# Two small loads of a fused FFN kernel issued from ScalarE instead of SyncE

## The chip, the cores and the metric

The kernel runs on one core of one Trainium2 chip. A core has five engines with instruction streams of their own: TensorE (PE in the profile, its weight loads PEld), VectorE (DVE), ScalarE (ACT), GpSimd (POOL) and SyncE (SP). They meet through semaphores. DMAs are issued by SyncE, GpSimd or ScalarE and carried by the core's 16 DMA engines. The metric is the time of one execution on the device in microseconds (us); lower is better.

## The reference

For each of 32 batch entries (here: tiles) of a 128 x 2048 input, a small MLP turns a conditioning vector into a softmax over 8 experts; the 8 expert matrices (128 x 128) are mixed with it and applied to the tile, with a mixed bias. A quantized SwiGLU feed-forward block (gate, up, down) follows, and its result is added to the input.

```python
h = gelu(embedding @ W0 + b0)
h = gelu(h @ W1 + b1)
att = softmax((h @ W2 + b2), axis=-1)                  # 32 x 8
agg_w = einsum('bk,koi->boi', att, weight[..., 0])     # mixed experts
out = einsum('boi,bih->boh', agg_w, x) + (att @ bias_k)[:, :, None]
# then, on 4096 rows of 2048: q, s = dynamic_quant(row * inv)
inter = clip(silu(gate(q)) * up(q))                    # 2048 -> 1024
x = x + down(dynamic_quant(inter))                     # 1024 -> 2048
```

## The kernel before, in words

Five instruction streams are written out by hand, one function per engine inside `adaln_ffn`; each stream's order is the order of its lines, and waits on named semaphores join them. A tile is one batch entry: 128 rows of 2048. For each tile TensorE runs conv (mixed expert matrix times input, L566), gate and up products (L613) and down (L716), interleaved over neighbouring tiles.

The start is the part that matters here. SyncE's stream opens with its loads, L340 to L352: `mlp_s` (L340: the conditioning vectors, the MLP's matrices and biases in one block of 153 KB), `b2_s` (L341: the 8 logit biases, copied to all 128 partitions), `wexp` (L342: the expert matrices, 512 KB, one row of 4 KB per partition), input 0 (L343, 1 MB), `invg_bc` (L344, 1 MB, one row copied to all partitions), inputs 1 and 2 (L345, L346), four row loads (L347 to L350) and, behind a wait for the first gate weights, input 3.

With the MLP block there, TensorE computes the two hidden layers (L511, L514) with ScalarE's Gelu between them (L920, L922). TensorE then waits for b2 (L516) and adds it with a one-row matmul (L518), logits follow (L521, L523), VectorE takes the maximum (L1016, L1018) and ScalarE the exponential (L924). The mixed expert matrix of tile 0 is made by two engines: VectorE sums experts 0 to 4 (`dve.wait_ge(wexp_in, 16)`, then L1069, L1072), TensorE experts 5 to 7 (L537) with diagonal matrices from ScalarE (L833), and VectorE adds both (L1077). ScalarE scales the experts for tile 1 (L837). conv(0) waits for that sum and for input 0. VectorE's bias sum (L1045) releases GpSimd's diagonal matrix (L461); GpSimd then waits for input 0 and issues the four gate weight loads (L432).

ScalarE's stream begins with a wait for the first hidden product and the Gelu. The compiler puts a table load (ACT_TABLE_LOAD) in front of that, and another one in front of the exponential. ScalarE issues no DMA. While TensorE waits early on, it runs filler matmuls (L505) whose result nobody reads.

Of the kernel before, what the change touches and what calls it, by code (L numbers as in the profile page):

```python
# [5 lines left out]
def adaln_ffn(nc, x, mlp, b2, weightT, w_gateT, w_upT, w_downT, inv_gate, rows, out):  # L6
# [6 lines left out]

    P = 128
    B, _, H = x.shape
    K = b2.shape[0]
    HID = 128
# [15 lines left out]
    with ctx:  # L33
        def sb(name, shape, dt=fp32):
            return ctx.enter_context(nc.sbuf_tensor(name, shape, dt))
# [4 lines left out]
        def sem(name):  # L40
            return ctx.enter_context(nc.semaphore(name))
# [10 lines left out]
        wexp = sb("wexp", [P, K, P])  # L52
# [70 lines left out]
        def qiT_at(t):  # L123
            if t == B - 1:
                return qgT[:, 0:KI * P]
            return QIT_HOME[t] if t < 2 else qiT[:, :]
# [29 lines left out]
        b2_s = qiT32[:, P + 3 * B:P + 3 * B + K]  # L156
# [35 lines left out]
        b2_in = sem("b2_in")  # L192
        wexp_in = sem("wexp_in")
# [126 lines left out]
        def xslot(t):  # L320
            return xt[:, (t % XS) * H:(t % XS + 1) * H]
# [16 lines left out]
        def _(sp):  # L338

            sp.dma_start(mlp_s, mlp).then_inc(mlp_in, 16)  # L340
            sp.dma_start(b2_s, b2.partition_broadcast(P)).then_inc(b2_in, 16)  # L341
            sp.dma_start(wexp[:, :, :], weightT).then_inc(wexp_in, 16)  # L342
            sp.dma_start(xslot(0), x[0, :, :]).then_inc(x_in[0], 16)  # L343
            sp.dma_start(invg_bc[:, :], inv_gate.partition_broadcast(P)).then_inc(invg_in, 16)  # L344
            sp.dma_start(xslot(1), x[1, :, :]).then_inc(x_in[1], 16)  # L345
# [445 lines left out]
        def _(act):  # L791
# [123 lines left out]
            def fix_i(t):  # L915
                act.wait_ge(iturned, 16 * t)
                nc.scalar.activation(qiT_at(t), qiT_at(t).bitcast(fp16), ACT.Copy, bias=-ROUND).then_inc(qiT_ready, 1)  # L917

            act.wait_ge(hid_mm, 1)
            nc.scalar.activation(h1, hid_ps, ACT.Gelu, bias=b0_s).then_inc(hid_act, 1)  # L920
            act.wait_ge(hid_mm, 2)
# [480 lines left out]
```

## Time and profile before

| | us |
|---|---|
| median of 3 runs | 803.78 (803.5 to 803.93) |
| the profiled execution | 803.78 |
| its span, first to last instruction | 802.0 |
| TensorE busy | 794.1 |
| VectorE busy | 715.4 |
| ScalarE busy | 441.1 |
| GpSimd busy | 147.9 |

A row of the timeline gives start, duration, engine, line, operation and tiles, and in brackets how long the engine sat idle before it and what released it; SPq is SyncE's stream of DMA issues, and its duration is that of the issue, not of the transfer. The chain rows give start, duration and what was on the chain. The time "to landing" runs from the start of an issue to its semaphore. The DMA view cuts a stretch into 40 slices and gives for each the busy tenths of the 16 DMA engines and the rate in GB/s.

### The profile page before, as it was taken

How to read it: one execution, taken by the hardware profiler on the slowest of the kernel's cores; microseconds unless marked ns; L12 is line 12 of the kernel's file. 1: busy time of each engine (PE TensorE's matmuls, PEld its weight loads, DVE VectorE, ACT ScalarE, POOL GpSimd, SP SyncE). 2: the span in 40 equal slices, each digit the busy share in tenths (PEclk: the TensorE clock that was granted, in tenths of full speed). 3: DMA queues.
4: the chain of work that ended last, by engine and by line, in shares of the span. 5: the costliest groups of instructions: out<-in, count | busy, mean ns of one | idle time of the engine just before them, and what ended most of it. 6: DMA issues, size and time to landing. Idle time of an engine off the chain costs nothing.

```text
span 802.0 us, 9186 instructions
## 1 busy us (share of the span) xinstructions
PE 794.1 (99%) x3521; PEld 365.3 (46%) x3521; DVE 715.4 (89%) x810; ACT 441.1 (55%) x385; POOL 147.9 (18%) x138
## 2 busy tenths in 40 slices
PE   8999999999999999999999999999999999999997
PEld 5554444444444444444444444444444444444443
DVE  6897899999888998888998888998888988888968
ACT  7774335555664545664545654555654546655531
POOL 2703210210122220122220122210222210222000
PEclk9999999999999999999999999999999999999999
DMA  8998745454445444445444445445455444454342
GB/s 300 225 215 172 161 142 171 149 166 125 131 138 171 145 145 120 129 145 170 145 145 122 119 154 167 147 145 112 122 161 161 154 129 136 108 167 154 90 111 105
DMA packets 162964, 119.81 MB, mean 149 GB/s; under 512 B 151780, under 2 KB 152164, under 8 KB 153703
## 3 DMA queue, kind: packets, MB, share of 16 engines
q1 hardware_dynamic: 161192, 106.64, 44.6%
q0 software_dynamic: 1728, 12.58, 7.8%
q8 instruction: 28, 0.46, 0.2%
q14 instruction: 16, 0.13, 0.1%
HBM read 60.48 MB, written 33.55 MB: 117 GB/s over the span
## 4 chain that ended last, share of the span: by engine, by line
PE 88%; DVE 7%; ACT 2%; issue 1%; DMA 1%; DVEq 0%; ACTq 0%
PE gate_ps L613 26%; PE up_ps L613 25%; PE down_ps L716 22%; PE conv_ps L566 12%; DVE amax L1092 2%; PE gate_ps L716 1%; DVE region L1150 1%; DVE xt L1265 1%; DVE down_sc L1256 1%; ACT qg L820 0%; DMA qgT<-qg 0%; PE up_ps L566 0%; PE down_ps L571 0%; ACT y L809 0%; DVE region L1219 0%
## 5 line engine op out<-in xcount | busy, mean ns | idle before, releaser
L716 PE MATMUL down_ps<-wd,qiT 128*128 128x512 bf16 x896 | 211.2, 379 | 0.0
L613 PE MATMUL gate_ps<-wg,qgT 128*128 128x512 bf16 x928 | 205.7, 379 | 0.0
L613 PE MATMUL up_ps<-wu,quT 128*128 128x512 bf16 x896 | 202.4, 379 | 0.0
L1092 DVE TENSOR_REDUCE amax<-region 128x1 f32<-128x2048 f32 (+1 forms) x90 | 173.0, 1922 | 1.2
L442 POOL TENSOR_TENSOR prod<-wexp,att_bc 128x1024 f32<-128x1024 f32 x28 | 53.1, 1898 | 540.9 <-DVE region L1150 498.3
L716 PEld LDWEIGHTS down_ps<-wd,qiT 128*128 128x128 bf16 x896 | 87.6, 98 | 123.4 <-issue 28.5
L613 PEld LDWEIGHTS gate_ps<-wg,qgT 128*128 128x128 bf16 x928 | 90.8, 98 | 109.4 <-issue 1.1
L613 PEld LDWEIGHTS up_ps<-wu,quT 128*128 128x128 bf16 x896 | 87.7, 98 | 106.1 <-ACT quT L885 0.4
L820 ACT ACTIVATE qg<-region,recip 128x2048 f16<-128x2048 f32 x30 | 60.1, 2002 | 128.9 <-DVE recip L1102 128.9
L566 PE MATMUL conv_ps<-xt,aggw 128*128 128x512 f32 x244 | 116.9, 602 | 0.8 <-ACT y L809 0.5
L809 ACT ACTIVATE y<-conv_ps,aggb 128x512 bf16<-128x512 f32 x116 | 78.9, 686 | 59.6 <-PE conv_ps L566 55.0
L1256 DVE SCALAR_TENSOR_TENSOR down_sc<-down_ps,scale,swd_bc 128x512 f32<-128x512 f32 x117 | 86.8, 742 | 0.2 <-PE down_ps L716 0.2
L1265 DVE TENSOR_TENSOR xt<-xt,down_sc 128x512 f32<-128x512 f32 x122 | 84.1, 690 | 3.2
L1203 DVE SCALAR_TENSOR_TENSOR region<-up_ps,scale,swu_bc 128x1024 f32<-128x1024 f32 x28 | 35.9, 1283 | 49.7 <-PE up_ps L613 49.7
L917 ACT ACTIVATE qiT<-qiT 128x1024 bf16<-128x1024 f16 x29 | 30.6, 1056 | 80.1 <-DMA qiT<-qi 80.1
L850 ACT ACTIVATE qu<-region,recip 128x2048 f16<-128x2048 f32 x30 | 60.1, 2003 | 18.6 <-DVE recip L1102 18.6
L566 PEld LDWEIGHTS conv_ps<-xt,aggw 128*128 128x128 f32 x244 | 46.3, 192 | 41.5 <-issue 29.8
L1147 DVE TENSOR_TENSOR region<-y,invg_bc 128x2048 f32<-128x2048 bf16 x27 | 61.7, 2284 | 0.0
L1150 DVE TENSOR_TENSOR region<-y,invu_bc 128x2048 f32<-128x2048 bf16 x27 | 61.7, 2283 | 0.0
L879 ACT ACTIVATE qgT<-qgT 128x2048 bf16<-128x2048 f16 x27 | 51.6, 1910 | 6.8 <-DMA qgT<-qg 6.8
L887 ACT ACTIVATE quT<-quT 128x2048 bf16<-128x2048 f16 x27 | 51.3, 1901 | 2.5 <-DMA quT<-qu 2.5
L899 ACT ACTIVATE qi<-region,recip 128x1024 f16<-128x1024 f32 x30 | 34.2, 1141 | 16.5 <-DVE recip L1102 16.5
(180 smaller groups left out, 582.1 us busy)
## 6 DMA issues: line engine op xcount, KB each, us to landing
xt<-x SPq DMA_DIRECT2D x30, 1024.0 KB, 4.8
out<-xt SPq DMA_DIRECT2D x29, 1024.0 KB, 4.0
wg<-w_gateT POOLq DMA_DIRECT2D x4, 1024.0 KB, 17.8
wu<-w_upT POOLq DMA_DIRECT2D x4, 1024.0 KB, 15.0
wd<-w_downT POOLq DMA_DIRECT2D x4, 1024.0 KB, 9.6
xt<-x SPq DMA_DIRECT2D x4, 512.0 KB, 4.8
invg_bc<-inv_gate SPq DMA_DIRECT2D x1, 1024.0 KB, 8.2
out<-xt SPq DMA_DIRECT2D x2, 512.0 KB, 2.9
```

The costliest lines, as they stand in the source:

```text
L442: nc.gpsimd.tensor_tensor(prod[:, :, :], wexp[:, :, :], a, ALU.mult).then_inc(pagg_step, 1)
L566: nc.tensor.matmul(conv_bank(t, c), aggw[t % 2][:, :], xcols(t, c), start=True, stop=True).then_inc(conv_done, 1)
L613: last = nc.tensor.matmul(acc[:, n * BANK:(n + 1) * BANK], codes[:, k * P:(k + 1) * P], wts[:, k, n * BANK:(n + 1) * BANK], start=(k == 0) ...
L716: last = nc.tensor.matmul(down_bank(t, c), qiT_at(t)[:, k * P:(k + 1) * P], wd[:, k, c * BANK:(c + 1) * BANK], start=(k == ks[0]), stop=(k ...
L809: nc.scalar.activation(y_at(t)[:, c * BANK:(c + 1) * BANK], conv_bank(t, c), ACT.Identity, scale=norm, bias=aggb[:, t:t + 1]).then_inc(y_r ...
L820: nc.scalar.activation(qg[:, :], xg_at(t), ACT.Copy, scale=trecip(t, 0), bias=ROUND).then_inc(gcodes_ready, 1)
L850: nc.scalar.activation(qu[:, :], xu_at(t), ACT.Copy, scale=trecip(t, 1), bias=ROUND).then_inc(ucodes_ready, 1)
L1092: nc.vector.tensor_reduce(amax[:, i:i + 1], src, axis=AX.X, op=ALU.max, apply_absolute_value=True).then_inc(max_ready, 1)
L1147: nc.vector.tensor_tensor(region1[:, :], y[:, :], invg_bc[:, :], ALU.mult).then_inc(xg_ready, 1)
L1150: nc.vector.tensor_tensor(region2[:, :], y[:, :], invu_bc[:, :], ALU.mult).then_inc(xu_ready, 1)
L1256: nc.vector.scalar_tensor_tensor(down_sc[c % 2], down_bank(t, c), tscale(t, 2), swd_bc[:, c * BANK:(c + 1) * BANK], ALU.mult, ALU.mult).th ...
L1265: nc.vector.tensor_tensor(result_at(t, c), xcols(t, c), down_sc[c % 2], ALU.add).then_inc(result_ready, 1)
```

## The change

The loads of `b2_s` and `wexp` are taken out of SyncE's stream, where they stood between the MLP block and input 0, and put at the head of ScalarE's stream, before its first wait. They go out through ScalarE's own DMA queue. Their destinations and semaphores stay the same, and so does everything that waits for them.

```diff
@@ -338,8 +338,6 @@
         def _(sp):
 
             sp.dma_start(mlp_s, mlp).then_inc(mlp_in, 16)
-            sp.dma_start(b2_s, b2.partition_broadcast(P)).then_inc(b2_in, 16)
-            sp.dma_start(wexp[:, :, :], weightT).then_inc(wexp_in, 16)
             sp.dma_start(xslot(0), x[0, :, :]).then_inc(x_in[0], 16)
             sp.dma_start(invg_bc[:, :], inv_gate.partition_broadcast(P)).then_inc(invg_in, 16)
             sp.dma_start(xslot(1), x[1, :, :]).then_inc(x_in[1], 16)
@@ -916,6 +914,8 @@
                 act.wait_ge(iturned, 16 * t)
                 nc.scalar.activation(qiT_at(t), qiT_at(t).bitcast(fp16), ACT.Copy, bias=-ROUND).then_inc(qiT_ready, 1)
 
+            act.dma_start(b2_s, b2.partition_broadcast(P)).then_inc(b2_in, 16)
+            act.dma_start(wexp[:, :, :], weightT).then_inc(wexp_in, 16)
             act.wait_ge(hid_mm, 1)
             nc.scalar.activation(h1, hid_ps, ACT.Gelu, bias=b0_s).then_inc(hid_act, 1)
             act.wait_ge(hid_mm, 2)
```

## Rows read from the trace of the kernel before

**Rows 1.** The page: span, busy time by engine, the chain by engine.
```profile
span 802.0 us, 9186 instructions
...
PE 794.1 (99%) x3521; PEld 365.3 (46%) x3521; DVE 715.4 (89%) x810; ACT 441.1 (55%) x385; POOL 147.9 (18%) x138
...
PE 88%; DVE 7%; ACT 2%; issue 1%; DMA 1%; DVEq 0%; ACTq 0%
```
**Rows 2.** The chain in order of time, 0 to 50 us: start, us, what.
```profile
0.73 2.26 DMA region<-mlp
...
6.41 0.24 ACT att_bc L924
...
7.28 1.63 PE gate_ps L537 x6
...
9.01 0.30 DVE aggw L1077
...
9.45 3.53 PE conv_ps L566 x4
```
**Rows 3.** Busy time by stretch: engines, granted clock, DMA share, GB/s.
```profile
9.45:97.00 87.55, 87.30 (x466) 44.61 (x467) 77.10 (x82) 53.13 (x56) 31.73 (x27) 1.00 0.93 208
```
**Rows 4.** The timeline of SyncE's issues, from the start.
```profile
0.73 0.39 SPq L340 DMA_DIRECT2D region<-mlp  x1
1.18 0.42 SPq L341 DMA_DIRECT2D qiT<-b  x1
1.65 0.42 SPq L342 DMA_DIRECT2D wexp<-weightT  x1
2.12 0.43 SPq L343 DMA_DIRECT2D xt<-x  x1
2.59 0.43 SPq L344 DMA_DIRECT2D invg_bc<-inv_gate  x1
```
**Rows 5.** The DMA view, issues up to 3 us: KB each, us to landing.
```profile
region<-mlp SPq DMA_DIRECT2D x1, 153.0 KB, 2.3
qiT<-b SPq DMA_DIRECT2D x1, 4.0 KB, 2.8
wexp<-weightT SPq DMA_DIRECT2D x1, 512.0 KB, 4.2
xt<-x SPq DMA_DIRECT2D x1, 1024.0 KB, 6.3
invg_bc<-inv_gate SPq DMA_DIRECT2D x1, 1024.0 KB, 8.2
```
**Rows 6.** The DMA view in 40 slices, 2 to 3 us, then 3 to 4.
```profile
GB/s 49 147 49 98 98 49 490 98 490 147 490 245 490 245 392 294 297 203 207 161 57 103 53 53 4 3 4 4 3 4 3 1 1 5 3 1 4 166 4 169
DMA packets 208, 0.13 MB, mean 135 GB/s; under 512 B 105, under 2 KB 206, under 8 KB 208
...
GB/s 4 4 4 1 1 9 3 4 4 494 328 4 1 165 3 1 165 0 3 1 3 165 329 0 165 0 1 1 164 0 164 0 0 0 492 328 164 328 328 0
DMA packets 78, 0.10 MB, mean 96 GB/s; under 512 B 55, under 2 KB 55, under 8 KB 78
```
**Rows 7.** The timeline of ScalarE up to its first activation.
```profile
0.72 1.28 ACT L920 ACT_TABLE_LOAD   x1 [0.72 <-PEq L1396]
...
3.71 0.29 ACT L920 ACTIVATE region<-gate_ps,region 128x32 f32<-128x32 f32 x1 [1.70 <-PE gate_ps L511]
```
**Rows 8.** The timeline where b2 and wexp are first used, and the last sum.
```profile
4.61 0.63 PE L518 MATMUL up_ps<-qiT 1*128 1x32 f32 x2
...
6.68 0.29 DVE L1069 TENSOR_SCALAR aggw<-wexp,att_bc 128x128 f32<-128x128 f32 x1 [0.30 <-ACT att_bc L924]
...
9.01 0.29 DVE L1077 TENSOR_TENSOR aggw<-aggw,gate_ps 128x128 f32<-128x128 f32 x1 [0.19 <-PE gate_ps L537]
```
**Rows 9.** The timeline of GpSimd before the gate weight loads.
```profile
9.90 1.90 POOL L461 TENSOR_TENSOR region<-ident,att_bc 128x1024 f32<-128x1024 f16 x1 [8.18 <-DVE aggb L1045]
...
11.74 2.35 POOL L432 DMA_DIRECT2D wg<-w_gateT  x4
```

## Prediction

> **What bounds the kernel now.** I read the page's busy line and chain first. TensorE is busy for 794.1 of 802.0 us, and 88% of the chain that ended last is its matmuls [rows 1]. So a change to a few loads at the start can only pay if TensorE's useful work begins sooner, or if a later stall of it goes. The next view is the chain in order of time: it begins with the DMA of the MLP block (issue to landing 0.73 to 2.99 us), runs through the small MLP, the exponential at 6.41 and the aggregation of expert weights on TensorE at 7.28 and on VectorE at 9.01, and reaches conv(0), the first large matmul, at 9.45 [rows 2]. The table of stretches then shows what stands behind it: between 9.45 and 97 us TensorE is busy for 87.30 of 87.55 us [rows 3]. Two things follow. Whatever moves conv(0) moves the end by the same amount, because there is no idle time to soak it up. And whatever only makes data land sooner after 9.45 is worth at most the 0.25 us of idle time in that stretch. The profiled execution stands at 803.78 us, 1.78 beyond its span of 802.0, and equals the median of the three runs shown, so a shift in the span can be added to 803.78 directly.
>
> **Part 1: two issues leave SyncE.** SyncE issues one DMA per 0.47 us (starts at 0.73, 1.18, 1.65, 2.12, 2.59) [rows 4]. Two go, so input 0 is issued at 1.18 instead of 2.12, and everything behind it, inv_gate, inputs 1 and 2 and the four row loads, up to 0.94 us sooner. Who needs this? Input 0 now lands at 2.12 + 6.3 = 8.4 us [rows 4, 5] and conv(0) starts at 9.45, released by the VectorE sum that ends at 9.31 [rows 2]. It has about 1 us to spare, so its gain is nothing. GpSimd also waits for input 0 before it issues the gate weights, but its diagonal matrix, released by VectorE, runs from 9.90 to 11.80 in front of that, and the first issue is at 11.74 [rows 9]; again nothing. inv_gate lands at 2.59 + 8.2 = 10.8 [rows 4, 5], before y(0) exists. The bulk stream being ahead is worth 0 to 0.25 us; I take 0, the value nearest to what these releasers show.
>
> **Part 2: two issues enter ScalarE ahead of its table load.** ScalarE's first instruction is the table load, 0.72 to 2.00, and its first Gelu starts at 3.71, behind the first MLP matmul [rows 7]. No row shows a DMA issue on ScalarE; the nearest are SyncE's, 0.39 to 0.43 us each at a spacing of 0.47 [rows 4]. Two of them put the table load at 0.72 + 0.94 = 1.66, ending at 2.95, with 0.75 us left before the Gelu. The cover is thus 0.75 us of waiting for the MLP block; it would be gone if one issue took more than about 0.8 us, twice what SyncE's take. Cost: 0. The second table load (for the exponential) is not touched.
>
> **Part 3: the bias row beside the MLP block.** The row (b2) needs 128 tiny packets. In the slices between about 2.65 and 3.7 us the core's DMA engines carry 3 to 5 GB/s most of the time, with 105 packets under 512 B in one microsecond and 55 in the next: that is b2, some 1.25 us long from about 2.45 to 3.7, although it holds next to no bytes [rows 6]. Now it is queued behind the MLP block and cannot hurt it. After the change both are issued at about 0.72, on two queues of the same engines. Bounds: 0, if tiny packets slip between the block's, to +1.25 us, if the whole of b2 goes first; below 0 is excluded since nothing stands before the block now. I take +0.1: the block moves its bytes at 300 to 490 GB/s in the same slices in which b2's first packets already run [rows 6]. b2 itself is wanted at 4.61 and lands at 1.18 + 2.8 = 3.98 [rows 4, 5, 8]; issued earlier it stays in time.
>
> **Part 4: the expert weights beside input 0.** This is the part on the path. The weights (wexp, 512 KB) now land at 1.65 + 4.2 = 5.85 us [rows 4, 5]; VectorE first uses them at 6.68 and then waits 0.19 us for TensorE before the last sum at 9.01 [rows 8], so they may land as late as 6.68 + 0.19 less a few hundredths of reaction, 6.84, before conv(0) moves. TensorE wants them at 7.28 only [rows 2]. Their lead today comes from order: they stand in front of input 0 in one queue. After the change they stand on another queue beside input 0. The rate: input 0 and inv_gate land 10.8 - 8.4 = 2.4 us apart, 1 MB (1.05 million bytes) each, so 0.42 to 0.43 MB/us. The MLP block's bytes are through at about 2.65 and it lands at 2.99, 0.35 later. If packets alternate between the queues (input 0's rows are 8 KB, wexp's 4 KB), wexp gets a third of the rate. When does it start? b2 is in front of it on its own queue; b2's quiet stretch begins at 2.45, 1.27 us after its issue at 1.18, and lasts 1.25 us, so from an issue at 0.72 it ends at 0.72 + 1.27 + 1.25 = 3.25. By then input 0 has moved for 0.6 us, 0.25 MB of its 1.05; the other 0.80 passes with 0.40 of wexp in 1.20/0.42 = 2.85 us, to 6.1, and wexp's last 0.12 takes 0.9 us at a third of the rate beside inv_gate, to 7.0. Landed 7.35, so +0.5 us. The same sum with b2 ending a quarter of a microsecond sooner or later gives some +0.25 or +0.75. I take +0.5. Bounds: 0 (wexp is served first; it then lands no later than its 5.85 of now) to +2.4 us (b2 is stretched until input 0 is through at 2.65 + 2.5 = 5.15, and wexp's 0.52 MB at a third of the rate takes 3.75 more: 8.9, landed 9.25, against 6.84).
>
> The delays of parts 3 and 4 don't add: the block's delay also moves the need for wexp. conv(0) moves by the larger, +0.5. Sum: 0 + 0 + 0.5 on 803.78 gives 804.3 us.
>
> The Trainium skill ("DMA: Bandwidth & Descriptors", section "Queues, rings and completion order") says that each DMA engine switches between queues only at packet boundaries, a packet being typically 9 to 17 descriptors, so a 128-row load's share of one engine would go out whole. By that rule wexp waits for input 0 at most once, the first rival below. The same page's section "Issuing engines are not separate DMA queues" says that issuing from several engines saves only the sequencer's issue time, which speaks against any gain here. No row of this trace shows SyncE's and ScalarE's queues side by side, since ScalarE issues nothing.
>
> **Rivals.**
> - Whole loads in turn, nothing late. Input 0 first, then wexp: 1.57 MB from 2.65 is done at 6.4, landed 6.7, before 6.84. Result 803.8 (803.5 to 804.0). For it: it needs only the bytes and the rate, and lands 0.14 us inside the limit. Against: the limit is close, and any packet of inv_gate or pause of b2 in front of wexp's last row breaks it.
> - The MLP block is late (part 3) by more than 0.2 us and sets the shift: about +0.6, 804.4. For it: b2's packets hold the engines nearly idle for a microsecond. Against: its packets are tiny.
> - On the other side, slower: wexp starved. The mechanism is b2 stretched by input 0's 8 KB packets, so that wexp meets inv_gate instead; it decides once wexp lands after 6.84, and passes 0.2% (1.6 us) at a landing of 8.45. At the bound it gives +2.4, 806.2; I price it at 805.9.
> - Faster: the earlier bulk stream removes idle time of TensorE I don't see as DMA. At most -0.25 in the stretch of [rows 3]; 803.5. A gain above 1.6 us has no row behind it.
> - The change doesn't do what it says: issues on ScalarE are far slower than SyncE's (past 0.8 us each), or a second issuing engine adds time outside the span. Table load and wexp late together: +1 to +2, 805.3.
>
> **How the numbers follow.** Forecast (wexp late by 0.2 to 1.4) 0.42; whole loads in turn 0.24; MLP block late 0.14; starved 0.09; earlier stream 0.05; slow issues 0.06. 0.2% is 1.6 us, about what a measurement of this kernel can tell from no change. Within it lie the forecast, the first two rivals, most of the small gain and half of the slow issues: 0.86. Slower: 0.09 + 0.03 = 0.12 less some starved cases that stay inside, 0.11. Faster: 0.03 for what no row shows. The range 803.2 to 805.7 takes in all but the starved case and part of the last.
>
> **What would show it.** In the changed kernel's timeline: SyncE issues input 0 near 1.2; ScalarE's two issues start near 0.72 and the table load ends before 3.1 with the Gelu still behind TensorE. In the chain: if the MLP block lands by 3.1, part 3 is right; if VectorE's first use of wexp is released by the wexp DMA near 7.3, and not by the exponential, part 4 is right; conv(0) at 9.9 to 10.0 confirms the sum. conv(0) at 9.45 means whole loads in turn. The forecast is wrong if conv(0) stays put and the time still moves by over a microsecond, or if TensorE's idle time between conv(0) and 97 us is no longer near 0.25 us.

## The result and the profile after

| | before | after |
|---|---|---|
| median of 7 runs, us | 803.85 (803.50 to 804.45) | 806.97 (806.15 to 807.79) |
| ratio | | 1.0037, 95% interval 1.0028 to 1.0046 |
| profiled execution, us | 803.78 | 806.23 |
| its span, us | 802.0 | 804.4 |

The change costs 3.1 us by the medians (2.3 to 3.7 by the interval) and 2.4 us between the two profiled executions, all of it inside the span: what lies around it is 1.8 us in both.

The page after, lines that answer to [rows 1]. TensorE's busy time rose by 0.9 us, and a DMA has a percent of the chain by line that it did not have:

```profile
span 804.4 us, 9186 instructions
PE 795.0 (99%) x3521; PEld 365.4 (45%) x3521; DVE 715.3 (89%) x810; ACT 441.1 (55%) x385; POOL 147.8 (18%) x138
PE 88%; DVE 7%; ACT 2%; DMA 2%; issue 1%; ACTq 0%; DVEq 0%
```

The chain after in order of time answers to [rows 2]. It doesn't begin with the MLP block any more but with the expert weights, 1.17 to 8.45 us, and reaches conv(0) at 11.02 instead of 9.45:

```profile
1.17 7.28 DMA wexp<-weightT
...
8.54 0.30 DVE aggw L1069
...
10.61 0.28 DVE aggw L1077
...
11.02 3.75 PE conv_ps L564 x4
```

The stretch of 87.55 us from conv(0) on, as in [rows 3], is as full as it was:

```profile
11.02:98.57 87.55, 87.30 (x463) 44.45 (x464) 76.22 (x82) 52.39 (x53) 31.69 (x27) 1.00 0.89 195
```

The issues, the table load and the first uses, in the timeline after, answer to [rows 4, 7, 8]. The two issues on ScalarE take 0.40 and 0.46 us and the table load ends at 2.94, as worked out. The MLP block is there at 3.78 (3.01 before), and VectorE now waits 1.40 us for the expert weights, where it waited 0.30 for the exponential:

```profile
0.73 0.39 SPq L340 DMA_DIRECT2D region<-mlp  x1
0.73 0.40 ACTq L917 DMA_DIRECT2D qiT<-b  x1
1.17 0.46 ACTq L918 DMA_DIRECT2D wexp<-weightT  x1
1.18 0.42 SPq L341 DMA_DIRECT2D xt<-x  x1
...
1.66 1.28 ACT L920 ACT_TABLE_LOAD   x1 [1.66 <-PEq L1396]
...
3.78 0.17 DVE L1005 COPY qiT<-region 128x8 f32<-128x8 f32 x1 [2.12 <-DMA region<-mlp]
...
8.54 0.29 DVE L1069 TENSOR_SCALAR aggw<-wexp,att_bc 128x128 f32<-128x128 f32 x1 [1.40 <-DMA wexp<-weightT]
```

The DMA view after, 4 to 7 us. q1 is SyncE's queue and carries input 0 in rows of 8 KB; q10 is ScalarE's and carries the expert weights in rows of 4 KB. They move 100 and 95 packets in these 3 us, and in each half microsecond of them 15 to 19 and 15 to 17: the engines take them in turn, row by row, and the expert weights get a third of the bytes (0.39 of 1.21 MB).

```profile
DMA packets 195, 1.21 MB, mean 403 GB/s; under 512 B 0, under 2 KB 0, under 8 KB 95
## 3 DMA queue, kind: packets, MB, share of 16 engines
q1 hardware_dynamic: 100, 0.82, 65.4%
q10 hardware_dynamic: 95, 0.39, 35.8%
```

And 2 to 4 us. Of the 0.31 MB on q1 the MLP block is about a half, and q10 moves little more than the bias row:

```profile
q1 hardware_dynamic: 143, 0.31, 67.9%
q10 hardware_dynamic: 149, 0.02, 6.1%
```

**Where the time between the two records went.** conv(0) starts 1.57 us later, but the second aggregation on TensorE (L537, after L535) starts at 20.36 instead of 17.96, 2.40 later; the last matmul ends up 2.44 later. So 0.83 us arise between the start of conv(0) and the second aggregation, with no wait. The timeline's weight loads show it. Before, they come every 0.86 us until 12.14 and every 0.43 us from 12.81 on:

```profile
11.29 0.34 PEld L566 LDWEIGHTS conv_ps<-xt,aggw 128*128 128x128 f32 x1 [0.52 <-issue]
12.14 0.34 PEld L566 LDWEIGHTS up_ps<-xt,aggw 128*128 128x128 f32 x1 [0.52 <-issue]
...
13.24 0.19 PEld L566 LDWEIGHTS up_ps<-xt,aggw 128*128 128x128 f32 x1 [0.24 <-issue]
```

After, the pace changes only at 16 us:

```profile
14.57 0.33 PEld L564 LDWEIGHTS up_ps<-xt,aggw 128*128 128x128 f32 x1 [0.52 <-issue]
...
15.42 0.33 PEld L564 LDWEIGHTS up_ps<-xt,aggw 128*128 128x128 f32 x1 [0.52 <-issue]
...
16.07 0.19 PEld L564 LDWEIGHTS up_ps<-xt,aggw 128*128 128x128 f32 x1 [0.32 <-issue]
```

Same instructions at half the pace: that is the ratio of TensorE's two levels, 1.2 and 2.4 GHz. The granted-clock column shows 1.00 for these stretches, so here the level has to be read from the spacing. What TensorE did before differs: it stood idle for 3.76 of the first 10 us, against 2.73. The Trainium skill ("TensorE: Matmul & The Clock Gate", Part 1) says that the engine runs at half clock after idling and that when it rises varies from run to run. The records agree on the second point above all. In a second record of the changed kernel (e11 below) the pace changes 1.7 us after conv(0) starts, where it took 5.1 in the first; in that record TensorE needs 7.68 us from conv(0) to the second aggregation, less than the kernel before (8.51):

```profile
11.77 0.34 PEld L564 LDWEIGHTS conv_ps<-xt,aggw 128*128 128x128 f32 x1 [0.52 <-issue]
12.46 0.19 PEld L564 LDWEIGHTS conv_ps<-xt,aggw 128*128 128x128 f32 x1 [0.35 <-issue]
```

So the 0.83 us belong to this record, and not to every execution of the changed kernel.

There is a second path. GpSimd's first row spread (PARTITION_BROADCAST: one row copied to all partitions) releases VectorE's inv_up product (L1127). Before, VectorE has 0.41 us to spare against TensorE at L1189; after, that wait is gone, because GpSimd stood idle for 11.38 us ahead of the spread instead of 10.01. Before:

```profile
24.10 2.30 POOL L453 PARTITION_BROADCAST invu_bc<-wu  x1 [10.01 <-issue]
...
45.29 1.28 DVE L1189 SCALAR_TENSOR_TENSOR down_sc<-gate_ps,scale,swg_bc 128x1024 f32<-128x1024 f32 x1 [0.41 <-PE gate_ps L613]
```

After:

```profile
27.04 2.30 POOL L451 PARTITION_BROADCAST invu_bc<-wu  x1 [11.38 <-issue]
...
47.74 1.28 DVE L1189 SCALAR_TENSOR_TENSOR down_sc<-gate_ps,scale,swg_bc 128x1024 f32<-128x1024 f32 x1
```

L1127 itself starts at 29.38 instead of 26.44, 2.94 later: 1.6 us because GpSimd's diagonal matrix starts later, as conv(0) does (11.48 against 9.90), and 1.4 us of longer idle time ahead of the spread. So the end moves by the larger of TensorE's shift at the second aggregation (2.40) and VectorE's shift at L1127 less about 0.5 us (2.44). In this record the two come out alike. Over the records below this holds to about 0.1 us, except in e4 (0.3 more), in e16 (0.8 more) and in e9, e10 and e12, whose transposes took longer.

### The profile page after: what moved, and what is told of

The parts are those of the page before. It is cut to its first block, busy times and chain, and to the rows that moved or that the text cites. A ratio compares the mean times of both kernels' runs of the same rounds, so it can differ in the third digit from the quotient of the medians.

```text
span 804.4 us, 9186 instructions
## 1 busy us (share of the span) xinstructions
PE 795.0 (99%) x3521; PEld 365.4 (45%) x3521; DVE 715.3 (89%) x810; ACT 441.1 (55%) x385; POOL 147.8 (18%) x138
## 4 chain that ended last, share of the span: by engine, by line
PE 88%; DVE 7%; ACT 2%; DMA 2%; issue 1%; ACTq 0%; DVEq 0%
PE gate_ps L611 26%; PE up_ps L611 25%; PE down_ps L714 22%; PE conv_ps L564 12%; DVE amax L1092 2%; DMA wexp<-weightT 1%; PE gate_ps L714 1%; DVE region L1150 1%; DVE xt L1265 1%; DVE down_sc L1256 1%; PE up_ps L564 1%; ACT qg L818 0%; DMA quT<-qu 0%; DMA qgT<-qg 0%; PE down_ps L569 0%
```

## The experiments

The landmarks of the profiled executions, in us from the span's start. "Block" is VectorE's first use of the MLP block, "experts" its first use of wexp, "agg 2" the second aggregation on TensorE, "spread" the start of GpSimd's first real spread with its idle time in brackets, "end shift" the start of the last matmul group against 796.67 before. The last column is the ratio of the runs to those of the kernel before on the same chip, with its interval. The medians of the kernel before were 803.6 to 803.8 us there.

| kernel | block | experts | conv(0) | agg 2 | spread | end shift | median | ratio |
|---|---|---|---|---|---|---|---|---|
| before | 3.01 | 6.68 | 9.45 | 17.96 | 24.10 (10.01) | 0 | 803.85 | 1 |
| after | 3.78 | 8.54 | 11.02 | 20.36 | 27.04 (11.38) | 2.44 | 806.97 | 1.0037 |
| e11, after again | 4.28 | 8.30 | 10.78 | 18.46 | 26.70 (11.28) | 2.01 | 805.77, one run | |
| e1, bias on ScalarE | 4.48 | 8.14 | 10.91 | 19.82 | 27.38 (11.83) | 2.71 | 805.82 | 1.0023 (1.0015 to 1.0032) |
| e2, experts on ScalarE | 4.52 | 8.60 | 11.37 | 19.45 | 27.24 (11.22) | 2.55 | 806.32 | 1.0030 (1.0018 to 1.0042) |
| e3, one queue, experts late | 2.95 | 8.62 | 11.10 | 19.60 | 25.76 (10.01) | 1.68 | 806.35 | 1.0029 (1.0019 to 1.0040) |
| e4, after, filled | 4.13 | 9.75 | 12.23 | 20.59 | 27.20 (10.33) | 2.91 | 806.01 | 1.0026 (1.0015 to 1.0037) |
| e5, issues held | 3.06 | 13.09 | 15.57 | 24.75 | 32.28 (12.07) | 7.67 | 810.78 | 1.0088 (1.0074 to 1.0102) |
| e6, before, filled | 3.06 | 6.72 | 9.49 | 17.81 | 23.58 (9.45) | -0.20 | 803.67 | 1.0001 (0.9992 to 1.0009) |
| e7, extra spread | 2.95 | 6.61 | 9.38 | 25.82 | 35.05 (9.29) | 10.33 | 814.11 | 1.0130 (1.0116 to 1.0144) |
| e8, before, unfilled | 3.04 | 6.70 | 9.47 | 18.85 | 23.51 (9.39) | 0.83 | 804.59 | 1.0009 (1.0000 to 1.0018) |
| e9, bias of one packet on ScalarE | 2.91 | 6.57 | 9.34 | 17.23 | 23.25 (9.27) | 1.94 | 805.44 | 1.0020 (1.0011 to 1.0029) |
| e10, the same, experts on ScalarE | 3.00 | 8.23 | 10.71 | 19.65 | 27.34 (11.98) | 4.13 | 807.42 | 1.0047 (1.0035 to 1.0060) |
| e12, the same, all on SyncE | 3.02 | 6.68 | 9.46 | 18.25 | 23.57 (9.47) | 1.84 | 805.62 | 1.0025 (1.0016 to 1.0034) |
| e13, one-row bias, SyncE | 3.10 | 6.76 | 9.53 | 18.61 | 23.60 (9.44) | 0.59 | 804.08 | 1.0002 (0.9993 to 1.0011) |
| e14, one-row bias, experts on ScalarE | 3.10 | 8.56 | 11.04 | 20.12 | 25.61 (9.93) | 2.13 | 806.16 | 1.0031 (1.0021 to 1.0042) |
| e15, input 0 held | 4.36 | 8.02 | 10.79 | 19.77 | 25.96 (10.53) | 1.75 | 805.52 | 1.0019 (1.0010 to 1.0027) |
| e16, one-row bias on ScalarE | 3.16 | 6.82 | 9.59 | 17.97 | 23.50 (9.26) | 0.82 | 804.26 | 1.0007 (0.9998 to 1.0015) |

**One part at a time.** e1 moves only the bias row, e2 only the expert weights:

```diff
 # e1: SyncE keeps wexp, ScalarE gets b2
-            sp.dma_start(b2_s, b2.partition_broadcast(P)).then_inc(b2_in, 16)
+            act.dma_start(b2_s, b2.partition_broadcast(P)).then_inc(b2_in, 16)
 # e2: SyncE keeps b2, ScalarE gets wexp
-            sp.dma_start(wexp[:, :, :], weightT).then_inc(wexp_in, 16)
+            act.dma_start(wexp[:, :, :], weightT).then_inc(wexp_in, 16)
```

> Only the bias row goes to ScalarE's queue; the expert weights stay with SyncE, in front of input 0. The theory (packets of two queues alternate, and whatever is in the other queue delays the MLP block) expects the block to land near 3.8 us as in the changed kernel, the expert weights before they are needed, conv(0) at 9.45 + 0.77 = 10.2, and a time 0.8 to 1.2 us above the kernel before. The rival (the block's delay came from input 0 and the expert weights pushing in, and the tiny packets are harmless) expects the block at 3.0 and the time of the kernel before.

> Only the expert weights go to ScalarE's queue, issued first there, at 0.73 us; the bias row stays with SyncE behind the MLP block. 
In e1 the block was there at 4.48 us, the expert weights made nobody wait, and conv(0) moved by just the block's delay, 1.46 us. I had expected the block at 3.8 and a loss of 0.8 to 1.2 us, and it is 2.1; the rival that calls tiny packets harmless is out. In e2 the block came at 4.52 and TensorE then waited for the bias, which stood behind the block, another 0.47 us. Both are slower on their own, by more than the forecast gave the whole change. In these two records the block's packets of 1.2 KB fare no better beside 32-byte than beside 4 KB packets.

**Late expert weights without a second queue.** e3 swaps two lines on SyncE's queue:

```diff
-            sp.dma_start(wexp[:, :, :], weightT).then_inc(wexp_in, 16)
             sp.dma_start(xslot(0), x[0, :, :]).then_inc(x_in[0], 16)
+            sp.dma_start(wexp[:, :, :], weightT).then_inc(wexp_in, 16)
```

> All loads stay with SyncE, but the expert weights are issued behind input 0 instead of in front of it. No second queue: the MLP block lands at 3.0 as before. The expert weights land where input 0 landed before, near 8.4 us, which is where they landed in the changed kernel. If the late expert weights are the whole price, VectorE's first use moves from 6.68 to about 8.5, conv(0) to about 11.0, and the time rises by 2.4 to 3.1 us like the changed kernel's. If the second queue or the late MLP block has a price of its own, the time rises by clearly less than that.

The block is on time, the experts are used at 8.62, conv(0) starts at 11.10, and the median rises by 2.6 us: late expert weights are enough for most of the loss.

**Filler in the changed kernel.** e4 adds matmuls whose result nobody reads:

```diff
-            fill(2, BANK)
+            fill(4, BANK)
...
+            fill(5, P)
             aggregate_mm(0)
```

> The changed kernel, with TensorE kept busy by more filler matmuls where it stood idle at the start: 4 of 512 columns instead of 2 ahead of the MLP block, and 5 more of 128 columns ahead of the aggregation of tile 0. The clock theory: after a wait TensorE runs the f32 passes of conv at 0.85 us spacing (the 1.2 GHz level) and only later at 0.43 (2.4 GHz), and the longer waits of the changed kernel put that change from 12.8 to 16.0 us; with the waits filled it comes earlier, at 14 us or before, and 0.5 to 1.7 us of the loss comes back with conv(0) still at 11.0. The rival: conv is slow because the loads write SBUF at over 400 GB/s at that time; then filler changes nothing and the spacing changes at 16 us again.

My conv(0) at 11.0 was wrong: the same loads landed at other times than in the record after (block 4.13, experts 9.75), so conv(0) was at 12.23. But from conv(0) to the second aggregation TensorE needs 8.36 us, against 9.34 in the changed kernel without the filler. The pace changes 3.2 us after conv(0) instead of 5.1. That isn't proof that the filler did it: e11, which has no added filler, needs only 7.68 us. The runs of this kernel lie between 804.3 and 809.4 us, so the median says little about the filler.

**The block's lateness.** e5 holds ScalarE's two issues back until VectorE's first memset is done:

```diff
+            act.wait_ge(filler_set, 1)
             act.dma_start(b2_s, b2.partition_broadcast(P)).then_inc(b2_in, 16)
```

> The changed kernel, but ScalarE waits for VectorE's first memset (1.5 us) before it issues its two loads, so they start 0.8 us after the MLP block's issue and not with it. If the block is late because the other queue has packets in the same microsecond, it lands at 3.0 to 3.2 us again. The expert weights lie beside input 0 and inv_gate as in the changed kernel and are issued later, so they land at 9 us or later, the table load ends at about 3.8, and conv(0) starts at 11.5 or later: the time is that of the changed kernel or up to 1 us above it. A rival theory, that the late block is what costs the time, expects a gain of 0.8 us or more against the changed kernel.

The block is on time (3.06) once the other queue's loads come 0.8 us later. The price moves on and grows: the bias row's 128 packets now meet input 0's 8 KB rows, and TensorE waits 4.67 us for 4 KB. The time is 810.8, where I had expected at most 1 us above the changed kernel. The mechanism is that of the rival that I had called starved, at three times its bound of 2.4 us. The row of e5's timeline:

```profile
9.40 0.60 PE L516 MATMUL up_ps<-qiT 1*128 1x32 f32 x2 [4.67 <-DMA qiT<-b]
```

**TensorE's pace in the kernel before.** e6 adds, e8 removes filler; no load is touched (e8's first removed line stands behind the first hidden layer):

```diff
 # e6
             fill(2, BANK)
+            fill(2, P)
...
+            fill(2, P)
             aggregate_mm(0)
 # e8
-            fill(3, P)
...
             aggregate_mm(0)
-            fill(3, P)
```

> The kernel before with 2 + 2 more filler matmuls of 128 columns in the two waits of TensorE at 2.6 and 6.8 us. The clock theory expects the step of conv's spacing from 0.85 to 0.43 us at 12.4 us or earlier instead of 12.8, and 0.4 to 0.9 us less until the second aggregation on TensorE. The theory of a second path (GpSimd's first row spread at 24.1 releases VectorE at 26.4, and VectorE then has only about 0.5 us to spare against TensorE near 45 us) caps what of it reaches the end at 0.5 us. So 803.3 to 803.8, hardly to be told from the kernel before. Without the second path the whole 0.9 us would show in the span.

> The kernel before without two groups of three filler matmuls (behind the first hidden layer, and between the aggregation and conv(0)). No load and no other engine is touched, so the MLP block, the expert weights and conv(0) at 9.45 stay. The clock theory expects the step of conv's spacing from 0.85 to 0.43 us later than 12.8, at 13.7 to 16.5, and each pass that starts before it to cost 0.43 us more: 0.4 to 1.7 us, 804.2 to 805.5. The rival (the spacing follows the loads into SBUF, not TensorE's history) expects 12.8 and 803.8 again.

e8 keeps conv(0) at 9.47 and changes pace at 14.6 us; the second aggregation is 0.89 us later and the end 0.83, and the median of its 11 runs is up by 1.0 us (interval 0.0 to 1.4, so barely clear of nothing). This speaks for a price of TensorE's own idle time, and against the rival by which the spacing follows the loads into SBUF, since no load was touched. A single record can't carry a figure, though: in the kernels whose conv(0) starts at 9.3 to 9.6 with all the filler in place (before, e9, e12, e13, e16) the pace changes 1.8 to 4.4 us after conv(0); e8's 5.1 lies just outside. e6 gains 0.15 us at the second aggregation, less than the 0.4 expected: the pace changed at 12.66. Its median is that of the kernel before.

**GpSimd's idle time.** e7 calls the spread once at the start and puts tile 2's diagonal matrix, which stood in front of the weight loads, behind them (those moved lines aren't shown):

```diff
+            nc.gpsimd.partition_broadcast(swd_bc[:, 0:P], ones[0:1, :]).then_inc(row_spread, 1)
             pool.wait_ge(x_in[0], 16)
             for i in range(WCH):
                 load(wg, w_gateT, i, wg_in)
...
```

> The kernel before with one extra small row spread (into columns that are written again later) at the start of GpSimd's stream, while it waits anyway, and with its diagonal matrix for tile 2 put behind the gate weight loads. It asks what the 10.0 us are that GpSimd stands idle ahead of its first spread. If that is the price of the first call of this operation, the extra call takes it at the start, and the real spread of inv_up starts near 16 us, when its row has landed, instead of 24.1; VectorE's wait of 1.93 us for it is gone. If the wait comes from the gate weight loads that GpSimd has just issued, the spread starts at 24 us as before. In both cases the end moves by less than 0.5 us, since TensorE's own path is the longer one: 803.3 to 804.0.

A clear miss, and both readings that I offered were wrong. The rows of e7's timeline:

```profile
9.72 0.43 POOL L460 PARTITION_BROADCAST swd_bc<-qiT  x1 [8.01 <-issue]
...
23.88 1.89 POOL L466 TENSOR_TENSOR region<-ident,att_bc 128x1024 f32<-128x1024 f16 x1 [11.40 <-issue]
...
35.05 2.30 POOL L453 PARTITION_BROADCAST invu_bc<-wu  x1 [9.29 <-issue]
```

GpSimd idles for 8.0 us ahead of the first spread, 11.4 us ahead of the next ordinary operation and 9.3 us ahead of the next spread: each change between the two kinds of work costs it, in both directions. The weight loads that it issues stand in front of the second of these only. A row of the kernel before speaks against them as the cause: right behind the issue of a weight load, with ordinary work before and after, GpSimd doesn't idle at all.

```profile
77.54 0.54 POOL L432 DMA_DIRECT2D wd<-w_downT  x1 [5.72 <-PE up_ps L613]
78.09 1.92 POOL L442 TENSOR_TENSOR prod<-wexp,att_bc 128x1024 f32<-128x1024 f32 x1
```

The second aggregation waits for the diagonal matrix until 25.82. VectorE's L1127 starts at 37.38, 10.94 later than before, and the end moves by 10.33 us: here the second path sets it.

**A bias of one packet.** e9, e10 and e12 give TensorE a one-partition copy of the bias and send the 128-partition copy later, behind input 2:

```diff
+        b2row = sb("b2row", [1, K])        # behind aggb
...
+            act.dma_start(b2row[0:1, :], b2.partition_broadcast(1)).then_inc(b2row_in, 16)   # e9, e10; sp. in e12
             sp.dma_start(xslot(2), x[2, :, :]).then_inc(x_in[2], 16)
+            sp.dma_start(b2_s, b2.partition_broadcast(P)).then_inc(b2_in, 16)
```

e9 and e12 leave the expert weights with SyncE, e10 has them on ScalarE's queue.

> The kernel before, but TensorE takes the logit bias from a one-partition copy of its own, which ScalarE loads (one packet of 32 bytes) beside the MLP block at 0.73 us; the 128-partition copy is issued by SyncE only behind input 2. A second queue is in use, but with one packet. If the block was late because packets of the other queue stand between its own on the same engines, it lands at 3.0 us, conv(0) starts at 9.45 and the time is that of the kernel before (803.3 to 804.3). If the mere use of a second queue, or building descriptors for two, delays the block, it lands at 3.4 or later and the time rises by 0.5 us or more.

> The changed kernel with the bias as a one-partition load of 32 bytes in front of the expert weights on ScalarE's queue, and the 128-partition copy behind input 2 on SyncE's. Nothing stands in front of the expert weights now, so they begin near 2.4 us instead of 3.8, alternate with input 0's 8 KB packets row by row and land near 7.0 instead of 8.5 us; the tail of the MLP block meets their 4 KB packets and it lands at 3.4 to 4.5. conv(0) at 10.0 to 10.9, time 804.5 to 806. If instead a load's share of an engine went out whole, the expert weights would land by 5.5 and the block alone would set the time.

> Everything stays on SyncE's queue, the bias as a one-partition load behind the MLP block and its 128-partition copy behind input 2. This takes the 1.25 us in which the engines carry next to nothing out of the front of the queue: the expert weights should land near 4.6 us instead of 5.85 and input 0 near 7.2 instead of 8.4. Both had 1 us to spare, so conv(0) stays at 9.45 and the time at that of the kernel before, 803.2 to 804.1. A gain of 0.5 us or more would say that the front of the queue has a price elsewhere that was not seen.

The early part came out as the packet theory says for the block, at 2.91 in e9 and at 3.00 in e10. For the expert weights in e10 it didn't: first used at 8.23, where I had them landing near 7.0. conv(0) was at 9.34 in e9, 10.71 in e10 and 9.46 in e12. But the medians were 805.44, 807.42 and 805.62 us, 1.8 to 3.8 above the kernel before. Against before, VectorE's instructions slip by another 1.5 us between 124 and 200 us in all three. In the steady part every DMA transpose takes longer. The DMA view of 250 to 700 us, kernel before:

```profile
qgT<-qg SPq DMA_TRANSPOSE x19, 3.7
quT<-qu SPq DMA_TRANSPOSE x19, 3.7
```

And e12:

```profile
qgT<-qg SPq DMA_TRANSPOSE x19, 4.3
quT<-qu SPq DMA_TRANSPOSE x19, 4.3
```

The three share a tile of 32 bytes in the middle of the layout, which moves all tiles behind it. e13, e14 and e16 are e12, e10 and e9 with that one line moved to the end:

```diff
-        b2row = sb("b2row", [1, K])        # behind aggb
...
         recip = sb("recip", [P, 12])
+        b2row = sb("b2row", [1, K])
```

> e12 (everything on SyncE's queue, bias row as a one-partition load) with its 32-byte tile placed behind all others, so that no other tile moves. If the place of the tiles made the DMA transposes 4.3 instead of 3.7 us long, they are 3.7 again and the 1.5 us that e12 lost between 124 and 200 us are back: 803.8 to 804.3. If the transposes suffer from the late bias copy or from the order of loads, they stay at 4.3 and the time at 805.6.

> e10 (the changed kernel with a one-packet bias row in front of the expert weights on ScalarE's queue) with that tile at the end. The MLP block should land at 3.0 again and the expert weights at 8.0 to 8.2, conv(0) at 10.7. By the layout theory the loss falls from 3.8 to about 2.3 us, 805.6 to 806.4: this is the price of the expert weights sharing with input 0, alone, with what follows from it on TensorE and GpSimd.

> e9 (a second queue that carries one packet beside the MLP block, the rest on SyncE's) with the tile at the end. Block at 2.9 to 3.0, conv(0) at 9.4, transposes 3.7 us long, time 803.6 to 804.4. If it stays above 805, the use of a second queue costs something apart from packets.

The transposes are back at 3.7 and 3.6 us and the times fall by 1.54, 1.26 and 1.18 us. It was the layout. In e16 a second queue with one packet costs 0.5 us by the medians (interval -0.2 to +1.2), not clear of nothing: conv(0) is at 9.59 and the second aggregation at 17.97, as before. Its end shift of 0.82 arises at gate(0), which starts 0.71 later. The late bias copy alone doesn't explain that: e13 has it too, and there gate(0) follows the second aggregation by the same 4.37 us as before, against 5.07 in e16. The cause stays open. e14 is the price of the experts' sharing alone, with the block on time: 2.4 us. Only one packet stood in front of the expert weights there, and still they came at 8.56.

**Input 0 held back.** e15 is the changed kernel with a wait in front of input 0:

```diff
+            sp.wait_ge(b2_in, 16)
             sp.dma_start(xslot(0), x[0, :, :]).then_inc(x_in[0], 16)
```

> The changed kernel, but SyncE issues input 0 only when the bias row has landed (near 3.9 us), so that the expert weights have the engines to themselves first. They should land at 5.5 to 6.2 instead of 8.5; the MLP block still meets the bias packets and lands at 3.8 to 4.3; input 0 lands near 8.5. Then conv(0) moves by the block's delay alone, 0.8 to 1.3 us instead of 1.6, and the time is 804.6 to 805.6. If the time stays at 806 or more, the sharing with input 0 was not what cost it.

The expert weights landed 4.5 us after their issue instead of 7.3 and no longer made anybody wait: VectorE's first use was released by the exponential. What is left, 1.8 us, is the block's delay (4.36) with its consequences.

**The record after, once more.**

> The changed kernel once more, for a second record of the same loads. If the landing times hang on how the packets of the two queues happen to meet, the MLP block and the expert weights land at other times than 3.8 and 8.45 us, by several tenths of a microsecond; with everything on one queue they repeated within 0.1.

The block came at 4.28 and the experts at 8.30, so the landings do hang on how the packets meet. In that record TensorE's pace changed early, at 12.5 us, so its own shift at the second aggregation is only 0.50, and the end was set by the second path: VectorE's L1127 at 29.04, 2.60 later than before, less 0.5, gives 2.1; the end shift is 2.01. The second path thus accounts for the end in both records of the changed kernel, TensorE's pace in one.

## Why the prediction was wrong, point by point

Two steps failed: Part 4's +0.5 us for the shift of conv(0), which measured 1.57, and the rule that the end moves by the same amount, where it moved by 2.44 in the record.

- **Half of the frame held.** Whatever moves conv(0) moves the end, but not by the same amount. Part 1's gain was nothing, and Part 2's cost too: the table load ended at 2.94 (forecast 2.95).
- **Part 3 was mis-sized.** +0.1 us for the block beside the bias row; it measured +0.77 in the record after, +1.27 in e11, +1.47 in e1 and +1.35 in e15. The argument for 0.1, that the block moves its bytes at full rate while the bias row's first packets already run, rested on one queue, where the block's packets come first. Beside another queue its last packets wait in turn with the other's. I took the wrong end of the bounds, 0 to 1.25, and three of these four records lie above the upper one.
- **Part 4 had the right mechanism and the wrong size.** Packets do alternate row by row. The rule of the Trainium skill ("DMA: Bandwidth & Descriptors", section "Queues, rings and completion order") as the prediction read it, that a load's share of an engine goes out whole, didn't hold here: q1 and q10 moved 100 and 95 packets in the same 3 us, about as many of each in every half microsecond. I put the landing at 7.35 and the cost at +0.5; it landed at 8.45, and conv(0) moved by 1.57. The latest harmless landing, 6.84, was right: 8.45 less 6.84 is 1.61. The third of the rate was right too: 0.39 MB in 3 us are 0.13 MB/us, against 0.14 in the sum. What was wrong was the start. I had the engines full from 2.65 us on, with 0.1 MB of the expert weights through by 4 us; q10 had moved 0.02 MB by then. e14 says that the bias row in front wasn't the reason: with one packet in its place the weights were first used at 8.56.
- **"The delays don't add" was right** for conv(0). In the record after, the block's 0.77 is hidden behind the experts' 1.57; e15 has the block's alone (conv(0) +1.34), e14 the experts' alone (+1.59).
- **A term was missing: TensorE's pace.** I took "conv(0) moves by x, the end moves by x". In the record after, the engine stayed at half the pace for longer, another 0.83 us. e8 speaks for it that idle time alone can cost that much (1.0 us by the medians, interval 0.0 to 1.4). That the changed kernel pays it in general isn't shown: e11 shows the opposite, with 0.83 us less than before between conv(0) and the second aggregation.
- **Another was missing: GpSimd and VectorE.** [rows 9] stop at the weight loads. The path behind them has 0.5 us to spare, and it set the end in e1, e2, e5, e7 and e11. In the record after it comes to 2.44 us, as much as TensorE's.
- **The rivals.** Whole loads in turn is out. The late block came true as an event, though not as what set conv(0). The starved case was given 0.09 at 805.9. That lies near the record's 806.23 by luck: it took 2.1 us from conv(0) alone, which moved by 1.57, and its mechanism (a stretched bias row that leaves wexp to meet inv_gate) didn't occur in the changed kernel. The bias row was stretched in e5.
- The sum on TensorE's path: 1.57 + 0.83 + 0.04 = 2.44 us in the record; on the second path: 1.6 + 1.4 - 0.5, about 2.4. The remaining 0.7 up to the median's 3.1 was not traced: the record is one of the low executions (806.23, where the seven runs reach 807.79), and e11 (805.77) is lower still. Both the landings and the pace differ between e11 and the first record, so either may make up the rest.

Two things stay open. Why GpSimd's idle time ahead of the spread is 9.3 to 10.0 us in the kernels with at most one packet on ScalarE's queue and 9.9 to 12.1 in the others; in e7 it was 8.0 ahead of the first spread, before GpSimd had issued any load of its own. And why both queues start slowly.

No version beat the kernel before.

## What to carry to other kernels

A load's place in one queue is a priority. Put on a queue of its own, it loses that: it shares with whatever the other queue carries, packet by packet, so small rows lose against big ones. Before moving a load, look at who reads its data first, and not at when it is issued. And where an engine's first work starts later, ask for the second-longest path, and take a second record before giving a figure to the engine's pace: here the one added what the first sum left out, and the other differed by 1.7 us between two records of one kernel.

## What the runs showed of the hardware that was not expected

- A 128-row DMA of 32-byte rows, issued at 1.55 us beside input 0 (issued at 1.19) on the other queue, took 7.7 us to land (e5), against 2.8 us in one queue [rows 5].
- GpSimd idles 8.0 to 12.1 us between a row spread and an ordinary operation, in either order (e7 and the table).
- A 32-byte tile in the middle of the layout made the transposes of 128 x 2048 2-byte values take 4.3 instead of 3.7 us, and those of 128 x 1024 3.1 instead of 2.7: 1.2 to 1.5 us of the whole.
- TensorE's f32 passes went at 0.86 or 0.43 us spacing while the granted clock stood at 1.00 in both.
